# Second attention of a fused kernel: rotation of q and k moved to later heads, and the first batch's partner transfers issued from two queues

## The reference, cut to what matters

```python
q, k, v = (proj(Wq), proj(Wk), proj(Wv))
q, k = _rope(q, k, s, d, hidden_states.dtype)      # x * cos + rotate_half(x) * sin
scores = einsum('bhqd,bhkd->bhqk', q, k) / math.sqrt(d)   # causal
tmp_sum = softmax(scores).sum(-2)                  # how much each key is attended to, per head
_, topk_idx = top_k(tmp_sum, heavy_budget)         # 25 heaviest keys of each head
scores = where(heavy_mask | band, scores, neg)
attn = softmax(scores) @ v
return attn @ Wo.T
```

## Time and profile before

| | us |
|---|---|
| median of 3 runs | 2262.65 (2259.99 to 2265.01) |
| the profiled execution | 2258.55 |
| its span | 2256.7 |
| second attention in it, from the first projection to the last | 46 to 743 |
| busy in the span: PE, DVE, ACT, POOL | 2000.1, 1312.0, 930.6, 219.9 |
| mean granted TensorE clock | 0.923 |

### The profile page before, as it was taken

The page is one execution under the profiler, slowest core; times in us unless marked ns, Lnnn a source line. Parts: engine busy times, 40 slices in busy tenths (PEclk is TensorE's granted clock), DMA queues, the critical chain, the costliest instruction groups (busy, mean ns, idle before and its releaser), DMA issues.

```text
span 2256.7 us, 84567 instructions
## 1 busy us (share of the span) xinstructions
PE 2000.1 (89%) x34605; PEld 1674.2 (74%) x34605; DVE 1312.0 (58%) x4974; ACT 930.6 (41%) x3362; POOL 219.9 (10%) x338
## 2 busy tenths in 40 slices
PE   5788888888889798866799999998999999999999
PEld 3455565565555677666789898998898988988987
DVE  3456465565576049755666666665666666666653
ACT  2253443543555122233444444443444444444432
POOL 0011011011011100000011011010110110110112
PEclk9789888899798898966899999999999999999999
DMA  6100000000000561200000000000000000000000
GB/s 248 31 6 16 19 6 15 16 10 15 17 8 2 194 231 56 88 3 17 18 17 4 27 18 18 13 18 19 27 4 18 27 4 27 18 18 13 4 12 10
DMA packets 61862, 74.95 MB, mean 33 GB/s; under 512 B 8480, under 2 KB 49888, under 8 KB 60608
## 3 DMA queue, kind: packets, MB, share of 16 engines
q1 hardware_dynamic: 59024, 54.82, 7.9%
q0 software_dynamic: 2448, 14.68, 1.9%
HBM read 44.27 MB, written 16.81 MB: 27 GB/s over the span
## 4 chain that ended last, share of the span: by engine, by line
PE 50%; DVE 5%; issue 2%; ACT 1%; DMA 0%; DVEq 0%; POOL 0%; ACTq 0%
PE ps L1374 26%; PE ps L1328 11%; PE ps L1308 10%; PE ps L1362 2%; PE ps L1317 1%; DVE hbuf L1544 1%; DVE dh L1532 1%; DVE dh L1538 1%; DVE cn L1522 0%; ACT nn L1441 0%; DVE hbuf L1541 0%; DVE cn L1510 0%; DVE hn L1525 0%; DVE h L1542 0%; DVE ns L1534 0%
## 5 line engine op out<-in xcount | busy, mean ns | idle before, releaser
L1374 PE MATMUL ps<-hbuf,whf 128*128 128x32 f16 x24480 | 657.9, 177 | 81.6 <-DVE hbuf L1544 59.0
L1374 PEld LDWEIGHTS ps<-hbuf,whf 128*128 128x128 f16 x24480 | 647.8, 96 | 104.2 <-DVE hbuf L1544 61.7
L1421 ACT ACTIVATE rz<-s,sc 128x32 f32<-128x32 f32 x512 | 164.5, 321 | 522.5 <-DVE s L1510 511.2
L1308 PE MATMUL ps<-hbuf,w1f 128*128 128x256 f16 x2304 | 292.7, 274 | 0.0
L1328 PE MATMUL ps<-hh,w2f 128*128 128x256 f16 x2304 | 292.1, 275 | 0.0
L1510 DVE TENSOR_REDUCE s<-ps 128x32 f32<-128x64 f32 x512 | 114.8, 224 | 273.4 <-PE ps L1374 260.0
L1497 POOL TENSOR_TENSOR hh<-tb,hh 128x256 f16<-128x256 f32 x192 | 132.4, 695 | 1302.1 <-ACT hh L1468 1302.1
L1308 PEld LDWEIGHTS ps<-hbuf,w1f 128*128 128x128 f16 x2304 | 224.1, 98 | 32.2 <-issue 6.0
L1328 PEld LDWEIGHTS ps<-hh,w2f 128*128 128x128 f16 x2304 | 211.4, 98 | 44.5 <-issue 19.9
L640 ACT ACTIVATE E<-ps,nm 128x128 f32<-128x128 f32 x256 | 94.9, 371 | 255.1 <-DVE nm L712 253.7
L1018 PE MATMUL ps<-x1T,wi 128*128 x768 | 173.9, 389 | 19.8 <-DMA wi<-in_W_ih 13.7
(11 more groups left out here) (192 smaller groups left out, 2824.6 us busy)
## 6 DMA issues: line engine op xcount, KB each, us to landing
gi_d<-stage SPq DMA_DIRECT2D x96, 128.0 KB, 1.7
gi<-gi_d SPq DMA_DIRECT2D x16, 768.0 KB, 5.1
swp<-raw SPq DMA_DIRECT2D x256, 32.0 KB, 1.9
w1f<-in_w1T POOLq DMA_DIRECT2D x4, 1408.0 KB, 9.0
xall<-in_x SPq DMA_DIRECT2D x4, 1024.0 KB, 9.0
x1T<-in_xT SPq DMA_DIRECT2D x1, 4096.0 KB, 22.0
w2f<-in_w2T POOLq DMA_DIRECT2D x2, 2048.0 KB, 10.5
out<-x1T SPq DMA_DIRECT2D x8, 512.0 KB, 3.1
```

The source lines that it names most:

```text
L1308: last = nc.tensor.matmul(ps[:, 6 + i % 2, 0:TT], w[:, wp, e % EH, c * P:(c + 1) * P], hbuf[par][:, k, hq, :, :].rearrange("p s b -> p (s ...
L1374: last = nc.tensor.matmul(ps[:, bank, g * WIDE * 2 * B:(g + 1) * WIDE * 2 * B], whp[:, k, w, q, g * P:(g + 1) * P], h[:, k, :, :].unsqueez ...
L1421: nc.scalar.activation(rz[:, q, :, :].rearrange("p g b -> p (g b)"), s1[:, q, :, :].rearrange("p g b -> p (g b)"), ACT.Sigmoid, scale=sc[: ...
```

## The change

`swap` becomes a function of the queue, and two things are different. The rotation steps move: unit 0 from slots 4, 5, 6 to 7, 8, 9; unit 1 from 7, 8, 9 to 10, 11, 12; unit 2 from 12, 13, 14 of the first pass to NH + 1, 2, 3 of the second; unit 3 from NH + 8, 9, 10 to NH + 10, 11, 12. And for batch 0 the 8 transfers of unit 1 are issued by ACT, behind its copy of that unit and ahead of its copy of unit 2; SP issues units 0, 2 and 3 there, and everything of the other batches as before. Projections and copies keep their slots.

```diff
--- before.py
+++ after.py
@@ -406,24 +406,26 @@
             if value > 0:
                 engine.wait_ge(semaphore, value)
 
+        def swap(queue, b, u):
+
+            i, p = UNITS[u]
+            x = raw[:, b % 2, i, 2 * p:2 * p + 2, :]
+            queue.wait_ge(a_raw, b * NU + u + 1)
+            passed(queue, v_rot, (b * NU + u - 1) * 3)
+            half = DH2 // 2
+            for to in range(0, P, half):
+                of = to + half if to % DH2 == 0 else to - half
+                queue.dma_start(swp[to:to + half, u % 2, :, :], x[of:of + half, :, :]).then_inc(d_swap[u % 2], 16)
+
         with nc.Block() as block:
             @block.sync
             def _(sp):
-                def swap(b, u):
-
-                    i, p = UNITS[u]
-                    sp.wait_ge(a_raw, b * NU + u + 1)
-                    passed(sp, v_rot, (b * NU + u - 1) * 3)
-                    x = raw[:, b % 2, i, 2 * p:2 * p + 2, :]
-                    half = DH2 // 2
-                    for to in range(0, P, half):
-                        of = to + half if to % DH2 == 0 else to - half
-                        sp.dma_start(swp[to:to + half, u % 2, :, :], x[of:of + half, :, :])\
-                            .then_inc(d_swap[u % 2], 16)
-
-                for b in range(B):
+                swap(sp, 0, 0)
+                swap(sp, 0, 2)
+                swap(sp, 0, 3)
+                for b in range(1, B):
                     for u in range(NU):
-                        swap(b, u)
+                        swap(sp, b, u)
 
             @block.gpsimd
             def _(pool):
@@ -671,6 +673,8 @@
 
                 for u in range(NU):
                     copy_raw(0, u, 4 + u)
+                    if u == 1:
+                        swap(act, 0, u)
                 for b in range(B):
                     for h in range(NH):
                         exps(b, 0, h)
@@ -831,7 +835,7 @@
 UNIT_BANK = (6, 6, 7, 7)
 PROJECT_AT = (0, 1, 3, 4, 7, 9, NH + 2, NH + 4)
 RAW_AT = (2, 5, 10, NH + 5)
-ROTATE_AT = (4, 5, 6, 7, 8, 9, 12, 13, 14, NH + 8, NH + 9, NH + 10)
+ROTATE_AT = (7, 8, 9, 10, 11, 12, NH + 1, NH + 2, NH + 3, NH + 10, NH + 11, NH + 12)
 CLOSE_AT = (12, 13)
```

## The result

2172.1 us (median of 4 runs, 2167.9 to 2178.0) against 2263.8 of the kernel before: ratio 0.9597, 95% interval 0.9568 to 0.9626. The prediction said 2174. The profiled execution took 2169.9 us, 88.6 less than the one of before.

The account below looks back on a forecast made before the run. In the second attention, DVE's waits for partner transfers stall PE, costing twice through its clock. Gains 2.8 + 60.1 + 10.9 + 23.8 - 11 = 86.6 off 2258.55 give 2171.9, stated as a 2174 us median; range 2152 to 2210.

Parts of the forecast that it names:

- First passes of batches 1 to 6: Second attention: with unit 1's wait gone PE runs through at full clock, each pass 41.1 us; gain 60.1 us.
- PE's stalls: Batch 4's first pass: PE idle for the second column sums' rdiag, an exponential and the last rdiag, 5.17 us.
- the slow work behind them: Batch 4's first pass: column sums, scores and close at PE's lower clock behind the idle stretch, 3.66 us.
- Batch 0: First pass of batch 0, which has no closes: DVE's chain decides, putting L604 10.9 us earlier.
- Second passes: Second passes of batches 0 to 6: DVE becomes the bound at 30.0 us; gain 23.8 us if the clock holds.
- falls of the clock: Second passes: two falls charged among seven batches, each at 35.6 less 30.0, -11 us.
- Before the first batch: Start, batch 0's transfers: unit 1 issued by ACT at SP's price lets units land earlier; gain 2.8 us.
- B: Rival: stalls go but the clock doesn't come back; gain some 45 to 55, 2207 to 2218 us; chance 0.14.
- the rule on transposes: Second passes: transposes don't count as PE activity like other matmuls, so a fallen clock would stay low.
- C: Rival: unit 2's steps beside POOL's diagonals delay transposes, so second passes gain nothing; 2189 to 2201 us; chance 0.14.
- D: Rival: DVE without slack keeps PE at 1.2 GHz through second passes; +66 us, 2328; chance 0.03.

Follow-up runs that it names:

- run 5: Changed kernel with units 0 and 1 back in slots 4 to 9, so only units 2 and 3 moved: 2234.4 us, ratio 0.9898 to the kernel before.
- run 6: As run 5, plus 8 matmuls nobody reads on PE in slot 10: 2223.0 us, ratio 0.9852 to the kernel before.
- run 8: Kernel before plus 8 matmuls nobody reads on PE in slot 10, ahead of the second column sums: 2277.9 us, ratio 1.0083.
- run 7: Changed kernel with unit 2's rotation in slots 13 to 15 of the first pass, behind unit 1's: 2180.8 us, ratio 0.9657 to the kernel before.
- run 3: Changed kernel with unit 0's rotation back in slots 4, 5, 6: 2176.3 us, ratio 0.9625 to the kernel before.
- run 9: Changed kernel with unit 2's three rotation steps directly behind DVE's copy of the heavy keys: 2176.1 us, ratio 0.9627 to the kernel before.
- run 11: Changed kernel with unit 2's steps behind the first pass's last rdiag, unit 3's in slots 1 to 3 of the next batch: 2157.8 us, ratio 0.9548.
- run 10: As run 9, plus unit 3's three steps in slots 1 to 3 of the next batch's first pass: 2172.7 us, ratio 0.9608 to the kernel before.
- run 12: As run 11, plus 2 matmuls nobody reads on PE in its wait for POOL's first masks: 2142.4 us, ratio 0.9495 to the kernel before.

## Why the prediction was right, point by point

**First passes of batches 1 to 6** (60.1): 60.2 measured, each length within 0.3 us of the 41.1 walked. The reason was half told. The text put the cost on PE's stalls (5.17) and the slow work behind them (3.66). Both are real (runs 5 and 6), but in the kernel before a second bound lay over the slow work: unit 2's wait of 5.04 us, through the last rdiag (run 8, where PE was 1.3 us sooner and waited 1.2 more). Runs 5 and 7 price the two: unit 2 moved without unit 1, 0; unit 1's wait gone, 6.7 (49.9 to 43.2); unit 2's behind it, 2.2 more. "The other waits of the first pass, for units 0 and 2, meet a PE that has projections and closes to do" was right for unit 0 (run 3) and wrong for unit 2. By that sentence moving unit 1 alone should have given all 8.8. That the sum came out is luck in this part: the change moved unit 2 out of the first pass as well, and the text counted nothing for it.

**Batch 0** (10.9): 9.9.

**Second passes** (23.8, less 11 for falls of the clock, 12.8): 21.5. The bound was right, DVE, as runs 9 and 11 show: with the steps away the pass is 1.7 to 2.6 us shorter at the same clock. The 30.0 us came out as 30.13. Two sizes inside it were off and went against each other: two of unit 2's three steps take 1.10 us beside POOL and not 0.6, and unit 3's wait is gone but for 0.76 us in batch 1. The falls were charged too high: two stretches of 3.4 us in batches 2 and 5, which cost 1.6 us each. Batch 0 gained 4.0 instead of 1.4, and the batches whose clock had been low (1, 2, 5) gained 5.0, 3.6 and 3.9 instead of 5.9, 5.3 and 5.6.

**Before the first batch** (2.8): 1.7. ACT issues at 0.611 us, 5.1 us for the eight, near SP's price as taken. But its copy of unit 2 came behind them at 61.85 and not at 61.2, later than the buffer was free, so it did cost something; that unit landed 1.3 us later than the walk had it, and unit 3 1.0 later.

**What lay outside the sum**: the last batch lost 2.0, by a stretch of low clock (587.3 to 594.1) that the kernel before didn't have, behind the same three PE waits in both (1.34, 0.77 and 0.62 us). The stretch behind the attention lost 2.7. The change doesn't touch it, and its length was 1513 to 1522 us in all the profiled executions of this document; the clock over the same 110 us of it was 0.60 instead of 0.70 (901.2 to 1011.2, and 992.5 to 1102.5 before). The gain as walked was 97.6 us and the measured one 88.6. The 9 us between them are the three misses above and these two losses, and the charge of 11 for falls in second passes met them by luck: 2174 said and 2172 measured is closer than the account earned.

**The rivals.** B, that the clock doesn't come back: refuted for first passes, all at 1.00 in batches 1 to 6. By the rule on transposes (the Trainium skill, TensorE: Matmul & The Clock Gate, PE-mode transpose) second passes would stay low once fallen; in batches 2 and 5 the clock fell and was back 3.4 us later, and batch 2 ran the rest of its pass at 1.00 with 27 transposes among its matmuls:

```profile
273.20:276.60 3.40, 3.40 (x34) 2.42 (x26) 1.35 (x6) 1.83 (x8) 0.00 (x0) 0.50 0.20 43
276.60:290.48 13.88, 11.77 (x129) 7.91 (x125) 12.74 (x49) 11.51 (x45) 1.19 (x2) 1.00 0.05 11
```

C, that DVE in the second pass gives all back: it bounds the pass, and its steps do slow beside POOL as that rival has it, and the pass still got shorter. D: no sign.

## What to carry to other kernels

Of several waits of one engine for transfers, ask for each what stands behind it in the same instruction stream and who waits for that: here 2.4 us of idle per batch cost next to nothing, and the waits for units 1 and 2 cost 8.9 between them, though the second one was hidden behind the first. Where removing a wait gives the expected time, check that it was the expected bound: of two bounds one behind the other, taking the hidden one away alone gave 0, the one in front alone 6.7, and both 8.9. Short waits of PE can cost more through the clock than in themselves, and a filler helps only where no other wait stands over the same stretch. Where there is no stall it is plain added work: look at every batch in which it is executed.

## What the runs showed that I hadn't expected

- **DVE beside POOL.** An element-wise operation of two 128x512 fp32 operands in SBUF takes 0.69 us, and 1.10 beside POOL's masks. Of the masks the slowest took 0.67 in the changed kernel and 1.06 in run 10, where most take 0.61. So DVE's only long idle stretch of the second pass was no free place for the steps: POOL is busy just there, PE waits for its first masks, and runs 9 and 10 gained nothing over the changed kernel.
- **The clock falls at short waits.** In the kernel before, each fall in the loop stood behind a wait of 2.5 us or more, the last batch apart. In run 10 it fell in every batch behind waits of 1.48 and 0.57 us; in run 11 behind 1.10 in two of six; with the wait cut to 0.24 (run 12) in none of the six. Such a wait alone doesn't settle it: the changed kernel has the 1.10 in every batch and fell in batches 1 to 6 only twice, each time behind waits of 0.90 and 0.99 further on; and in the last batch the same three waits went with a fall in one kernel and with none in the other.
- **A filler of the right size made the kernel before 17 us slower** (run 8). Some 7 of them are the last batch, which has no stall to fill; for the rest it stays open.
